# Layers 1 to 3 of a four-layer conditioned FFN made sparse: blocks of 128 slots, gathered rows, weights by computed expert

## The reference

```
c = bi_wkv(r=x, k=f, v=f, w, u, cond)     # sigmoid(x) times a ratio that does not depend on x
x = x + ffn_l(c)
```

## Time and profile before

| | us |
|---|---|
| median of 3 runs | 772.42 (772.38 to 773.41) |
| the profiled execution | 773.22 |
| its span, first to last instruction | 771.4 |
| TensorE (PE) busy | 639.2 |
| VectorE (DVE) busy | 581.6 |
| GpSimd (POOL) busy | 389.6 |
| ScalarE (ACT) busy | 262.8 |

### The profile page before, as it was taken

The page is one execution under the profiler, slowest core; times in us unless marked ns, Lnnn a source line. Parts: engine busy times, 40 slices in busy tenths (PEclk is TensorE's granted clock), DMA queues, the critical chain, the costliest instruction groups (busy, mean ns, idle before and its releaser), DMA issues.

```text
span 771.4 us, 9946 instructions
## 1 busy us (share of the span) xinstructions
PE 639.2 (83%) x3123; PEld 468.5 (61%) x3123; DVE 581.6 (75%) x947; ACT 262.8 (34%) x504; POOL 389.6 (51%) x299
## 2 busy tenths in 40 slices
PE   0030315999999889999998899999999996999997
PEld 0020314777778667777766577777777765666665
DVE  6999693999999746777756477777773367688785
ACT  1310042222222633333327333333333344444452
POOL 4733585999995325555523245555553223334433
PEclk9999999999999889999999899999999998799999
DMA  9000002555551102111111021111111111122211
GB/s 282 25 28 0 1 28 67 149 162 158 154 146 30 35 8 52 49 53 49 45 41 42 10 63 48 48 48 48 48 48 54 31 56 57 48 71 78 84 56 54
DMA packets 49281, 49.19 MB, mean 64 GB/s; under 512 B 4192, under 2 KB 40160, under 8 KB 49248
## 3 DMA queue, kind: packets, MB, share of 16 engines
q1 hardware_dynamic: 47520, 44.06, 19.4%
q0 software_dynamic: 1728, 4.72, 2.0%
HBM read 46.67 MB, written 2.10 MB: 63 GB/s over the span
## 4 chain that ended last, share of the span: by engine, by line
PE 72%; DVE 17%; POOL 4%; issue 3%; ACT 2%; DMA 1%; DVEq 0%; SPq 0%; POOLq 0%; ACTq 0%
PE y_ps L443 20%; PE g_ps L388 19%; PE u_ps L388 12%; PE y_ps L578 8%; PE u_ps L551 4%; PE g_ps L432 4%; POOL R L1386 3%; DVE fwd L895 2%; PE g_ps L566 2%; PE u_ps L432 2%; DVE fwd L884 2%; DVE bwd L885 2%; DVE w_lo L1213 1%; DVE A L1096 1%; PE r_ps L536 1%
## 5 line engine op out<-in xcount | busy, mean ns | idle before, releaser
L1333 POOL TENSOR_TENSOR h_lo<-h,h_hi 128x512 fp32r<-128x512 f32 x104 | 139.0, 1336 | 281.0 <-ACT h_hi L857 281.0
L857 ACT ACTIVATE h_hi<-h 128x512 fp32r<-128x512 f32 x104 | 65.7, 632 | 180.9 <-DVE h L1294 180.2
L1014 DVE TENSOR_TENSOR t<-act_g,u_ps 128x512 f32<-128x512 f32 x72 | 48.5, 673 | 94.9 <-PE u_ps L388 92.3
L443 PE MATMUL y_ps<-h_hi,w_hi 128*128 128x512 f32 x208 | 93.4, 449 | 0.5 <-ACT h_hi L857 0.5
L388 PE MATMUL g_ps<-c_hi,w_hi 128*128 128x512 f32 x208 | 87.6, 421 | 3.8 <-POOL c_lo L1333 1.3
L388 PE MATMUL g_ps<-c_lo,w_hi 128*128 128x512 f32 x208 | 84.9, 408 | 0.0
L388 PE MATMUL g_ps<-c_hi,w_lo 128*128 128x512 f32 x208 | 84.7, 407 | 0.0
L811 ACT ACTIVATE act_g<-g_ps 128x512 f32<-128x512 f32 x104 | 61.7, 593 | 66.0 <-PE g_ps L388 65.5
L443 PE MATMUL y_ps<-h_hi,w_lo 128*128 128x512 f32 x208 | 82.4, 396 | 0.0
L1347 POOL TENSOR_TENSOR fwd<-fwd,bwd 128x512 f32<-128x512 f32 x32 | 44.1, 1378 | 47.7 <-DVE bwd L885 47.6
L443 PE MATMUL y_ps<-h_lo,w_hi 128*128 128x512 f32 x208 | 66.0, 398 | 0.9 <-POOL h_lo L1333 0.9
(11 more groups left out here) (188 smaller groups left out, 1280.9 us busy)
## 6 DMA issues: line engine op xcount, KB each, us to landing
raw<-in_wglu SPq DMA_DIRECT2D x36, 320.0 KB, 2.9
wup<-in_wglu SPq DMA_DIRECT2D x36, 256.0 KB, 3.7
wdn<-in_wglu SPq DMA_DIRECT2D x12, 384.0 KB, 4.2
raw<-in_wglu SPq DMA_DIRECT2D x36, 128.0 KB, 2.1
raw_q<-in_wq SPq DMA_DIRECT2D x16, 256.0 KB
raw_s<-in_s_up SPq DMA_DIRECT2D x32, 64.0 KB
raw_s<-in_s_down SPq DMA_DIRECT2D x16, 128.0 KB
fs<-in_fT SPq DMA_DIRECT2D x2, 512.0 KB, 4.9
```

What stands on the lines that cost most here:

```text
L443: return pe.matmul(y_ps[:, m, hf, :], w[:, slot, DN0 + m * P:DN0 + (m + 1) * P], r[:, k % HB, :], start=start and first, stop=False, skip_ ...
L857: act.activation(h_hi[:, k % HB, :], h[:, k % 2, :], ACT.Copy).then_inc(h_hi_ready, 1)
L1014: dve.tensor_tensor(t[:, par, :], act_g[:, par, :], other, ALU.mult).then_inc(t_ready, 1)
L1333: return pool.tensor_tensor(dst, src, hi.bitcast(F32), ALU.subtract)
```

## The change

- Layers 1 to 3 no longer compute every expert for every token. The two choices of each token (`choose`, `gates_of`) become slots: each expert's choices are laid in blocks of 128 slots, and 2 x 8 + n - 1 blocks (23, 29 and 31, `BK`) are always enough. `positions2` (TensorE, bf16) counts, `slots` makes 0/1 tables A2 and B2, `lists2` (TensorE) turns them into a list of token numbers per block, `read_lists2` makes the row indices of the gather and of the scatter, and `block_experts` the expert number of each block (`be`).
- Per block: GpSimd gathers 128 rows of c (`gather2`), TensorE transposes (`block_turn`), ScalarE moves (`block_move`), TensorE multiplies up in f32 with no split (`block_up`), ScalarE applies silu or relu (`block_act`), VectorE multiplies (`block_hidden`), TensorE multiplies down (`block_down`), ScalarE copies out (`block_out`), GpSimd scatters the 128 rows into a DRAM buffer at 2 x token + choice (`scatter2`). SyncE reads the expert number from SBUF into a register (`value_load`) and loads that expert's weights into one of three buffers (`load_block`).
- After the blocks SyncE loads the buffer back in two halves of 1 MB (`ysb`), and TensorE multiplies it with diagonal matrices of the gates (`final`), which turns it back to channels on partitions and adds both choices to y.
- The shared experts of layers 1 and 2 are computed densely in f32 in six steps (`shared_up`, `shared_down`), four ahead of the blocks and two behind them.
- The gate and up weights of layers 1 and 2 are first copied from DRAM to DRAM into another layout (`wx`, 9.4 MB, eight DMAs of rows of 512 bytes, issued by ScalarE in the prologue). The 16 experts of layer 3 are unpacked beside blocks of layers 1 and 2 (`unpack`, `scale_w3`) and stored in DRAM (`w3`).
- The WKV units of layers 1 and 2 run in quarters behind blocks (`wkv_part`), all on VectorE but the differences.
- In the prologue the four parts of a WKV unit are summed on TensorE with the identity and its negative (`wkv_sums`), in f32; GpSimd only makes exp(u+k) v (`euk_v`) and its `add_u` ops come earlier. SyncE issues the six constants ahead of f's second half and x.

The parts of the diff that the prediction speaks of:

```diff
--- before.py
+++ after.py
+NE = [0, E1, E2, E3]
+BK = [0] + [2 * TT + n - 1 for n in NE[1:]]
+XB, OB, WB = 4, 3, 3
 @block.sync
+            def load_shared(layer):
+                first = NE[layer] * I1
+                wait(sp, shd_done, NSH * (layer - 1))
+                sp.dma_start(wsu[:, :, :], wx[layer][:, :, first:first + SH1]).then_inc(wsh_in, 16)
...
+            def load_block(layer, b):
+                n = B0[layer] + b
+                w = n % WB
+                wait(sp, bd_done, n - WB + 1)
+                e = sp.value_load(be[0:1, b:b + 1], min_val=0, max_val=NE[layer] - 1)
+                if layer < 3:
+                    sp.dma_start(wU[:, w, :, :], wx[layer][:, :, bass.ds(e * I1, I1)]).then_inc(w_in[w], 16)
+                    sp.dma_start(wD[:, w, :, :], flat[bass.ds(e * I1 + row0(layer), I1), DN0:DN0 + C]
+                                 .rearrange("(h i) n -> i h n", h=2)).then_inc(w_in[w], 16)
...
+                for b in range(WB, BK[layer]):
+                    e = unpacked(layer, b - WB)
+                    if e is not None:
+                        store_w3(e)
+                        if e + 2 < E3:
+                            load_q(e + 2)
+                    load_block(layer, b)
+                if layer == 1:
+                    load_shared(2)
+                for w in range(OB):
+                    sp.wait_ge(y_out[w], 16 * len(range(w, B0[layer] + BK[layer], OB)))
 @block.tensor
+            def wkv_sums(o):
...
+                wait(pe, R_ready, 3 * (o - 1))
+                pe.wait_ge(eukv_ready, o + 1)
+                add(num, ident_s, dif[:, buf, 0, :], True, False)
+                add(den, ident_s, unit(R, q), False, False)
+                pe.wait_ge(scan_ready, o + 1)
+                add(num, minus_s, unit(ekv, q), False, False)
+                add(den, minus_s, unit(ek, q), False, False)
+                add(bank, ident_s, fwd[:, buf, :, :].rearrange("p f n -> p (f n)"), False, False)
+                add(bank, ident_s, bwd[:, buf, :, :].rearrange("p f n -> p (f n)"), False, True
+                    ).then_inc(num_ready, 1)
...
+            pe.wait_ge(minus_ready, 1)
+            wkv_sums(0)
+            wkv_sums(1)
             renumber_gate()
+            wkv_sums(2)
+            wkv_sums(3)
+            logits0(0)
+            turn_c(0, 0)
+            wkv_sums(4)
+            positions(0)
...
+                if shared:
+                    shared_up(layer, 0)
+                    shared_up(layer, 1)
+                    shared_down(layer, 0)
+                positions2(layer)
...
+                block_turn(layer, 0)
+                for b in range(BK[layer]):
+                    if b + 1 < BK[layer]:
+                        block_turn(layer, b + 1)
+                    block_up(layer, b)
+                    if b:
+                        block_down(layer, b - 1)
 @block.scalar
             for hf in range(2):
                 sigmoid_x(0, hf)
+            for layer in (1, 2):
+                for q in range(2 * KT):
+                    act.dma_start(wx[layer][:, q, :].rearrange("p (c n) -> p c n", n=P),
+                                  wglu[sum(CH[:layer]):sum(CH[:layer + 1]), :, q * P:(q + 1) * P]
+                                  .rearrange("c p n -> p c n")).then_inc(wx_in, 16)
             act.wait_ge(gwt_done, 1)
             act.activation(gwn[:, :], r_ps[:, 0:C], ACT.Copy).then_inc(gwn_ready, 1)
 @block.vector
             for layer in range(1, NL):
...
+                for b in range(BK[layer]):
+                    block_hidden(layer, b)
+                    if layer < 3 and b < 4 * QN[layer]:
+                        wkv_part(Q0[layer] + b // 4, b % 4)
+                    e = unpacked(layer, b)
+                    if e is not None:
+                        unpack(e)
 @block.gpsimd
+                for b in range(BK[layer]):
+                    if b + XB - 1 < BK[layer]:
+                        gather2(layer, b + XB - 1)
+                    if layer < 3 and b < 4 * QN[layer] and b % 4 == 0:
+                        q = Q0[layer] + b // 4
+                        wait(pool, wkv_done, q - Q0[1] - 1)
+                        wkv_dif(q, q, q % UNITS, q % 2)
+                    if b:
+                        scatter2(layer, b - 1)
```

More of the change, by code:

```diff
@@ L15 @@
 UNITS = KT * NB
-HB = 4
 E0, KEPT, CAP, I0 = 128, 48, 96, 96
@@ L65, in wait, with unpacked @@
         eng.wait_ge(sem, value)
[L68 to L98, removed]
+def unpacked(layer, b):
+    e = 2 * (b // 4) + b % 4 + 2 * QN[1] * (layer - 1)
+    return e if layer < 3 and b % 4 < 2 and b < 4 * QN[layer] and e < E3 else None
 def build(nc, xT, fT, cond, wu, o2n_row, o2n_col, gwT, rconst, gscale, wglu, wq, s_up, s_down, sel3,
@@ new lines, in block_down @@
+            def block_down(layer, b):
+                n = B0[layer] + b
+                w, s = n % WB, n % 2
+                pe.wait_ge(bh_ready, n + 1)
+                wait(pe, o_ready, n)
+                dst = g_ps[:, 1, s * C:(s + 1) * C]
+                if layer < 3:
+                    for h in range(2):
+                        mm = pe.matmul(dst, h_s[0:IH, s, h, :], wD[:, w, h, :], start=h == 0, stop=h == 1,
+                                       skip_group_check=True)
+                else:
+                    mm = pe.matmul(dst, h_s[:, s, 0, :], w3b[:, w, C:2 * C], start=True, stop=True,
+                                   skip_group_check=True)
+                mm.then_inc(bd_done, 1)
@@ new lines, in final @@
+            def final(layer, hf):
+                pe.wait_ge(y_in[hf], 16 * layer)
+                pe.wait_ge(diag_ready, layer)
+                for i in range(TT)[of_half(hf)]:
+                    o = i % TH * P
+                    for m in range(KT):
+                        for j in range(2):
+                            mm = pe.matmul(y_ps[:, m, hf, o:o + P], ysb[:, i, j * C + m * P:j * C + (m + 1) * P],
+                                           diag[:, j, i, :], start=layer == 3 and i % TH == 0 and j == 0,
+                                           stop=i % TH == TH - 1 and j == 1, skip_group_check=True)
+                mm.then_inc(fin_done, 1)
@@ L605, in _ @@
+            lists(0)
+            wkv_sums(7)
+            logits0(1)
+            turn_c(0, 1)
+            positions(1)
+            lists(1)
             for b in range(BG):
@@ L657, in _ @@
-                steps(pe, layer, body, more=4)
+                shared = layer < 3
+                for hf in range(2):
+                    logits(layer, hf)
+                    turn_c(layer, hf)
+                if shared:
[3 more added lines that the diff above has]
+                positions2(layer)
+                if shared:
+                    shared_up(layer, 2)
+                    shared_down(layer, 1)
+                lists2(layer)
@@ new lines, in _ @@
+                shared = layer < 3
+                sigmoid_x(layer, 0)
+                sigmoid_x(layer, 1)
+                store_c(layer, 0)
+                if layer == 2:
+                    scores_silu(layer)
+                    store_c(layer, 1)
+                    router_exp(layer)
+                else:
+                    router_exp(layer)
+                    store_c(layer, 1)
+                if shared:
+                    for k in range(SHEAD):
+                        shared_silu(layer, k)
@@ L869, in _ @@
+                if shared:
+                    for k in range(SHEAD, NSH):
+                        shared_silu(layer, k)
         @block.vector
```

955 lines of the change are left out of this document (495 added, 460 removed).

## The result

The changed kernel takes 827.32 us, median of 4 runs (823.53 to 832.97), against 772.75 for the kernel before: 1.071 times as long, 95% interval 1.064 to 1.078. The prediction was 738, with a range of 690 to 820: the wrong sign, and outside the range. The profiled execution has a span of 821.7 us, 85.0 over the sum's 736.7.

A forecast was written before the change was run, and what follows sets the result against it. It took TensorE to bound layers 1 to 3, then each block's weight loads. Start 257.7 + prologue 16 + routing 102 + blocks 286 + return 75 = 736.7 us of span, hence 738 us; range 690 to 820.

The forecast's parts named there:

- What bounds the kernel before, and that TensorE's work leaves: Layers 1 to 3: TensorE bounds them, busy 490.0 of 513.7 us; after the change all blocks need 180 us of it.
- Routing, return, start of layer 1: Layers 1 to 3: exposed routing 102 us, outputs returned to y 75 us; layer 1 starts at 257.7 + 16.
- Prologue +16: Prologue: 16 us longer, about 5 from f32 sums on TensorE and 11 from ScalarE issuing eight DRAM to DRAM copies.
- The rival, 27 us and more held by data that moves: Prologue: the copies hold ScalarE for 27 to 54 us instead of 11; total 754 to 781, chance 0.17.
- Weights of a block: Blocks of layers 1 and 2: weight loads through three buffers set the pace, 3.4 us a block, between 2.8 and 5.4.
- L: Weight loading: time from a down product's end to the next weights' landing, taken as 4.25 us, between 2.95 and 8.25.
- up + down: Blocks of layers 1 and 2: TensorE's up and down products in the weight cycle, taken as 2.6 us.
- my list of what would break the forecast: Blocks: register load over 2 us, gathers queued behind 1 MB and weight loads, or TensorE at half rate (2.8 becomes 5.6).
- Unpacking, 0.75 us in 32 blocks: Layers 1 and 2: unpacking layer 3's weights adds 0.75 us a block, making 32 blocks 4.2 us and 20 blocks 3.4.
- GpSimd as the bound: Blocks: gathers and scatters at 1.86 us each need 4.2 or 3.7 a block; 786 us, chance 0.28 shared with late weights.
- the case of late weights: Blocks: weights arrive late; grouped with GpSimd as 786 us (776 to 830), joint chance 0.28.
- a held ScalarE: Prologue: ScalarE held by the eight copies until data moves, 754 to 781 us; chance 0.17, a third of it slower.

The follow-up runs named there:

- the early register load: Changed kernel with SyncE reading a block's expert number before, not after, it waits for the block's buffer: 798.6 us, 1.038 of the kernel before.
- the fourth buffer: Changed kernel with four weight buffers instead of three, nothing else: 766.5 us, 0.994 of the kernel before.
- the two waits: Changed kernel with up and down products each waiting for their own weight DMA on its own semaphore: 792.2 us, 1.029 of the kernel before.
- the run on three buffers without the unpacking: Changed kernel with early register load and separate up and down weight waits, layer 3 on other weights: 752.5 us, 0.972 of the kernel before.

## Why the prediction failed

- *What bounds the kernel before, and that TensorE's work leaves*: right, and not enough. TensorE's busy time in layers 1 to 3 fell from 490 to about 370 us, part of it at half the clock.
- *Routing, return, start of layer 1*: 102 forecast and 104 measured, 75 and 76, 273.7 and 276.3. The sums held, their terms only in part. Layer 3's return is right term by term: scatter and landing 4.4 (5.0), the load of y 5.5 (5.2 and 0.5 for the issue; no row shows the base of 2.2 in it), the products 9.4 (7.8). In layer 2 the agreement (21 and 20.2) is luck: its chain has neither scatter nor load, but 10.3 us of the last shared products, which the sum didn't have. In layer 1's routing the logits took 9.4 us with the transposes between them where 2.2 were charged, and shorter terms elsewhere make up for half of the difference.
- *Prologue +16*: measured +17.5 (145.1 - 127.65), near by luck: two errors cancel. For the sums on TensorE I charged a loss of 5, and the prologue without the copies is 4.6 shorter. For the copies I priced the issue by row count from SBUF loads (11 charged, 22 measured). The 0.45 ns a row doesn't follow from its own two rows: 0.16 us for 128 rows more is 1.25 ns a row, and by that the eight issues take 22. The rival, 27 us and more held by data that moves, comes as near: the eight issues took 25.4 us in the changed kernel and 26.2 when they stood behind gwp, and the 9.4 MB at the 348 GB/s of the earlier trace rows are 27. No run decides between rows and bytes.
- *Weights of a block*: the step that failed, (4.25 + 2.6)/2 = 3.4 us a plain block where 4.9 to 5.1 came. The structure was right: the early register load, the fourth buffer, the two waits and the run on three buffers without the unpacking bear it out. (The text names the down product of b-1 for the load of b+1; the code waits for that of b-2, `n - WB + 1` done, which stands in order just behind the up product of b-1. The cycle is the same.) Its terms were too small. L left out the issue of the block's first DMA ahead of its second (0.9). The landing was taken as the median of wup, 3.7, for twice the bytes (4.44), and the register load 0.2 too short. And up + down was taken at full rate (2.6 for 4.1): it was on my list of what would break the forecast, with no share in the chances. That last term depends on the others: a TensorE that waits 3 us in every other block loses its clock, which lengthens the cycle, which keeps the wait. The Trainium skill describes this (TensorE: Matmul & The Clock Gate, HAM oscillation — how this bites in real kernels): short tiles with a wait for a DMA in each lower the clock again and again. The traces agree, 0.88 against 1.00 for a wait that is 0.8 us shorter.
- *Unpacking, 0.75 us in 32 blocks*: about right for the kernel as it is (0.4 to 0.75), in part hidden behind the slow weights; once they are fast, 1.2 to 1.6 a block in layer 1 and 0.8 in layer 2.
- *GpSimd as the bound*: fell in layers 1 and 2. Its gathers came last there mainly where the weights were early (four buffers). Of the gathers of layer 0, 8 of 36 take 2.9 to 3.7 us, not one in three.
- *The range*: the case of late weights was there, as 786 with 830 at its top, and I cut it at 820. L up to 8.25 alone would have given 5.4 a block, near what came, though L was 6.1 and the clock did the rest; that bound stood in the text, belonged to the likeliest mechanism, and should have set the end of the range. The chances have a slip too: of the 0.17 for a held ScalarE a third was to be slower, but the sum counts a third as faster; by its own words faster had 0.66 and not 0.61.

## What to carry to other kernels

In a ring of n buffers, n - 1 items last at least as long as one refill plus one use (measured here for three; with four, gathers and TensorE itself came last before it), and the refill counts from the release: the register load, every DMA issued ahead of the one that is awaited, and the landing. Take what needn't follow the release out of it, wait for each part where it is used, and see whether SyncE has time for all its issues before giving it more. When a change turns a full TensorE into one that waits, price its products at half the clock first.

## What was not expected of the hardware

A wait shortened by 0.8 us gave 0.84 a block where the cycle alone gives 0.4, through the granted clock (0.88 to 1.00). Eight copies from DRAM to DRAM, 9.4 MB in rows of 512 B, hold the issuing engine for 26 us, 3.3 us each; from an issue to its landing it is 10.9 us in the median, and a load from DRAM to SBUF of 352 KB held SyncE for 0.57. An f32 product of 72 columns took as long as one of 128, 0.22 us.
